# First layer of a four-layer attention stack: residual of the feed-forward on TensorE, GpSimd's norm between its energies, two buffers for low products

## What is computed

```
def layer_norm(x, g, b): return (x - mean) / sqrt(var + 1e-5) * g + b
Qh = (queries @ Wq).reshape(n, t, 16, 16).swapaxes(2, 3)
Kh = (keys @ Wk).reshape(n, t, 16, 16)
Vh = (values @ Wv).reshape(n, t, 16, 16).swapaxes(2, 3)
energy = jnp.matmul(Qh, Kh) / 8, and -1e+20 for masked tokens
attn = softmax(energy, axis=-1)
x = layer_norm(jnp.matmul(attn, Vh).reshape(n, t, 256) @ Wo + queries, ln1_g, ln1_b)
ff = relu(x @ W1 + b1) @ W2 + b2
return layer_norm(ff + x, ln2_g, ln2_b)
```

## Time and profile before

| | us |
|---|---|
| median of 3 runs | 2060.57 (2059.95 to 2061.29) |
| the profiled execution | 2058.21 |
| its span | 2056.5 |
| busy PE / PEld / DVE / ACT / POOL | 1810.5 / 1346.7 / 1258.3 / 1082.0 / 987.9 |
| first layer, from the start to about | 362 |
| mean granted TensorE clock, share of full speed | 0.928 |

### The profile page before, as it was taken

The page is one execution under the profiler, slowest core; times in us unless marked ns, Lnnn a source line. Parts: engine busy times, 40 slices in busy tenths (PEclk is TensorE's granted clock), DMA queues, the critical chain, the costliest instruction groups (busy, mean ns, idle before and its releaser), DMA issues.

```text
span 2056.5 us, 34737 instructions
## 1 busy us (share of the span) xinstructions
PE 1810.5 (88%) x12417; PEld 1346.7 (65%) x12417; DVE 1258.3 (61%) x2220; ACT 1082.0 (53%) x3150; POOL 987.9 (48%) x1233
## 2 busy tenths in 40 slices
PE   4777886879879978979999999999999999999997
PEld 3666675646646646656667767677676676766766
DVE  5878888574464464464465675756746547455471
ACT  2222221475576566566456565655655556656563
POOL 5666777564364355355244464535543334333340
PEclk8999998888978878887999999999999999999999
DMA  6300000000200000000000200000000000000000
GB/s 185 130 6 11 6 6 6 6 1 6 87 1 6 6 1 6 6 1 6 6 1 6 88 7 6 1 7 6 6 7 1 6 6 6 22 6 1 11 2 11
DMA packets 31361, 35.92 MB, mean 17 GB/s; under 512 B 3196, under 2 KB 30040, under 8 KB 30808
## 3 DMA queue, kind: packets, MB, share of 16 engines
q1 hardware_dynamic: 31192, 33.70, 5.3%
HBM read 31.60 MB, written 2.10 MB: 16 GB/s over the span
## 4 chain that ended last, share of the span: by engine, by line
PE 61%; DVE 14%; ACT 11%; POOL 6%; issue 5%; SPq 3%; DMA 1%; DVEq 0%; POOLq 0%; ACTq 0%
PE ps L590 34%; PE ps L794 6%; PE ps L732 6%; PE ps L804 5%; PE ps L838 4%; ACT work L972 3%; ACT work L979 3%; DVE work L1167 2%; PE ps L603 2%; POOL work L1360 2%; DVE xn L1026 2%; DVE rowmax L1171 2%; PE ps L753 2%; PE ps L819 2%; ACT hT L887 1%
## 5 line engine op out<-in xcount | busy, mean ns | idle before, releaser
L590 PE MATMUL ps<-hT,w_slot 128*128 128x256 f32 x1696 | 409.6, 395 | 18.2 <-ACT hT L887 16.1
L1284 POOL TENSOR_TENSOR work<-KT,own_head 128x512 f32<-128x512 f32 x256 | 262.5, 1047 | 286.8 <-PE ps L794 179.8
L590 PEld LDWEIGHTS ps<-hT,w_slot 128*128 128x128 f32 x1696 | 322.8, 196 | 78.6 <-ACT hT L887 21.7
L979 ACT ACTIVATE work<-work,rowmax 128x128 f32<-128x128 f32 x768 | 245.0, 392 | 168.2 <-DVE rowmax L1171 167.5
L804 PEld LDWEIGHTS ps<-ident,work 128*128 128x128 f32 x1536 | 198.9, 153 | 170.8 <-issue 89.0
L972 ACT ACTIVATE work<-ps,rowmax,score_scale 128x128 f32<-128x128 f32 x512 | 229.1, 488 | 114.5 <-DVE rowmax L1175 114.1
L804 PE MATMUL ps<-ident,work 128*128 128x128 f32 x1536 | 265.3, 301 | 18.3 <-ACT work L979 17.3
L794 PE MATMUL ps<-work,QT 128*128 128x512 f32 x512 | 266.4, 605 | 9.6 <-POOL work L1284 4.6
L1360 POOL TENSOR_SCALAR work<-work,winv 128x128 f32<-128x128 f32 x512 | 185.6, 383 | 159.0 <-DVE winv L1187 156.6
L1201 DVE RECIPROCAL O<-ps 128x128 f32<-128x128 f32 x128 | 122.3, 955 | 176.1 <-PE ps L838 175.4
L965 ACT ACTIVATE work<-ps 128x512 f32<-128x512 f32 x256 | 150.6, 595 | 91.2 <-PE ps L804 91.2
(11 more groups left out here) (129 smaller groups left out, 3290.3 us busy)
## 6 DMA issues: line engine op xcount, KB each, us to landing
ctx_in<-in_ctx SPq DMA_DIRECT2D x32, 256.0 KB, 2.7
w_slot<-in_L_xattn_W SPq DMA_DIRECT2D x2, 1024.0 KB, 6.4
w_slot<-in_L_xattn_ff_w SPq DMA_DIRECT2D x1, 2048.0 KB, 10.9
w_slot<-in_L_xattn_ffn_w SPq DMA_DIRECT2D x2, 1024.0 KB, 9.3
w_slot<-in_L_xattn_w SPq DMA_DIRECT2D x2, 1024.0 KB, 8.9
out<-x_all SPq DMA_DIRECT2D x8, 256.0 KB, 2.1
x_all<-in_x SPq DMA_DIRECT2D x1, 1536.0 KB, 11.7
pad<-in_mask_Bx1x1xS_fk SPq DMA_DIRECT2D x1, 1024.0 KB, 8.5
```

The costliest lines, as they stand in the source:

```text
L590: mm = pe.matmul(dst, lhsT(k), rhs(k), start=(k == 0), stop=(k == chunks - 1))
L979: ex = act.activation(prob[i % NPF][:, tok(h)], src[:, tok(h)], ACT.Exp, bias=shifts[:, at:at + 1])
L1284: pool.tensor_tensor(KB[u % NK].rearrange("p (h k) -> p h k", h=HU), keys, own_head[:, e:HC:2].unsqueeze(2).broadcast_to([P, HU, S]), ALU. ...
```

## The change

Four things, all in layer one. (1) The first norm's `post` and the `bias` step go; x after the first norm is no longer written. Its place as residual is taken by a piece `res`: four products of hT (x1 transposed, with g and b) with the identity, which open the PSUM accumulation of y2, and the second `sum` adds the row b2 to PSUM and writes x. (2) On GpSimd A1 moves from step 1 to step 4, so the first norm's two instructions come between A0 and A1; on TensorE E1 moves from step 3 to step 8, on VectorE W0 ahead of S1, on ScalarE the second exp from step 7 to 8. (3) Low products have two buffers: B0 writes `prodA`, B1 `prodB`. So B1 no longer waits for L0, B0 waits for E1 (`E_low_ps`), and A0 for L0 of the phase before. B1 moves from step 10 to 9. (4) The last `post` moves from slot 6 to slot 9. Two rows fewer are loaded.

```diff
@@ -33,8 +33,8 @@
     [("ctx", {}), ("stage", {}), ("tin", {}), ("local", {}), ("out", {"w": "Wo"}),
-     ("norm", {"eps": 1e-5}), ("post", {"g": "L0_ln1_g", "b": "L0_ln1_b"}), ("tin", {"g": "L0_ln1_g", "b": "L0_ln1_b"}),
-     ("bias", {"v": "L0_b2"}), ("ffn", {"w1": "W1", "b1": "L0_b1", "w2": "W2", "act": "relu"}),
+     ("norm", {"eps": 1e-5}), ("tin", {"g": "L0_ln1_g", "b": "L0_ln1_b"}),
+     ("ffn", {"w1": "W1", "b1": "L0_b1", "w2": "W2", "act": "relu", "res": "L0_b2"}),
      ("norm", {"eps": 1e-5}), ("post", {"g": "L0_ln2_g", "b": "L0_ln2_b"})],
@@ -73,7 +73,8 @@
         n = FC if arg["act"] == "geglu" else FC // 2
-        return [(f"f{f}", (f % 2 == 2 - 1) + 0 * (f == n - 1)) for f in range(n)] + [("y2", 0), ("sum", 1)]
+        res = [("res", 1)] if "res" in arg else []
+        return [(f"f{f}", f % 2 and not (res and f == n - 1)) for f in range(n)] + res + [("y2", 0), ("sum", 1)]
     if kind == "norm":
@@ -142,7 +143,7 @@
-LOCAL_LEFT_SLOT = {"norm": 4, "scale": 5, "post": 6}
+LOCAL_LEFT_SLOT = {"norm": 4, "scale": 5, "post": 9}
@@ -229,7 +230,7 @@
-ROWS = ["L0_ln1_g", "L0_ln1_b", "L0_b2", "L0_ln2_g", "L0_ln2_b", "L1_a1_bo", "L1_a2_bo", "L1_ff_b2",
+ROWS = ["L0_b2", "L0_ln2_g", "L0_ln2_b", "L1_a1_bo", "L1_a2_bo", "L1_ff_b2",
         "L2_mha1_bo", "L2_mha1_bv", "L2_ln1_g", "L2_ln1_b", "L2_mha2_bo", "L2_mha2_bv", "L2_ln2_g", "L2_ln2_b",
@@ -550,10 +551,11 @@
         LOCAL_STEPS = {
-            "pe": {2: [0], 3: [1]},
-            "act": {6: [0], 7: [1]},
-            "dve": {0: [("A", 0), ("R", 0)], 4: [("A", 1)], 5: [("R", 1), ("S", 0)], 6: [("S", 1)], 7: [("W", 0), ("B", 0)], 8: [("W", 1), ("L", 0)], 9: [("B", 1)], 10: [("L", 1)]},
-            "pool": {0: [("A", 0)], 1: [("A", 1)], 7: [("B", 0)], 10: [("B", 1)]},
+            "pe": {2: [0], 8: [1]},
+            "act": {6: [0], 8: [1]},
+            "dve": {0: [("A", 0), ("R", 0)], 4: [("A", 1)], 5: [("R", 1), ("S", 0)], 6: [("W", 0), ("S", 1)], 7: [("B", 0)],
+                    8: [("W", 1), ("L", 0)], 9: [("B", 1)], 10: [("L", 1)]},
+            "pool": {0: [("A", 0)], 4: [("A", 1)], 7: [("B", 0)], 9: [("B", 1)]},
         }
@@ -570,7 +572,7 @@
             x = DH // 2
-            prod = (prodD if half else prodB).rearrange("p (x h y) -> p x h y", x=x, h=H)
+            prod = (prodD if half else (prodA, prodB)[j]).rearrange("p (x h y) -> p x h y", x=x, h=H)
             e = E[:, j, half * P:(half + 1) * P].rearrange("p (x y) -> p x y", y=DH).unsqueeze(2).broadcast_to([P, x, H, DH])
@@ -585,9 +587,9 @@
-            def product(dst, lhsT, rhs, chunks):
+            def product(dst, lhsT, rhs, chunks, onto=False, more=False):
                 for k in range(chunks):
-                    mm = pe.matmul(dst, lhsT(k), rhs(k), start=(k == 0), stop=(k == chunks - 1))
+                    mm = pe.matmul(dst, lhsT(k), rhs(k), start=(k == 0 and not onto), stop=(k == chunks - 1 and not more))
                 return mm
@@ -724,6 +726,12 @@
                             mm.then_inc(q["hid_ps"], 1)
+                    elif piece == "res":
+                        pe.wait_ge(q["hid_ready"], FC * use("ffn", layer, g, n["ffn"]) + FC - 2)
+                        for j in range(G):
+                            for k in range(C):
+                                pe.matmul(one[:, j * D + k * P:j * D + (k + 1) * P], hT[st][:, k, tok(j)], ident[:, :],
+                                          start=(j == 0 and k == 0), stop=False)
                     elif piece[0:2] == "y2" and len(piece) == 3:
@@ -736,7 +744,8 @@
                         for j in range(G):
-                            mm = product(one[:, j * D:(j + 1) * D], lambda k: hid[:, k, tok(j)], lambda k: w[arg["w2"]][:, k, :], FC)
+                            mm = product(one[:, j * D:(j + 1) * D], lambda k: hid[:, k, tok(j)], lambda k: w[arg["w2"]][:, k, :], FC,
+                                         "res" in arg, "res" in arg and j < G - 1)
                         mm.then_inc(q["y_ps"], 1)
@@ -1028,7 +1037,10 @@
                         dve.wait_ge(q["y_ps"], use("yadd", layer, g, n["yadd"]))
-                        if n["bias"]:
+                        if "res" in arg:
+                            dve.wait_ge(s["rows_loaded"], 16 * len(ROWS))
+                        elif n["bias"]:
@@ -1039,6 +1051,8 @@
                                 .then_inc(q["yadd_done"], G)
+                        elif "res" in arg:
+                            dve.tensor_tensor(xs, y, row(arg["res"]).unsqueeze(1).broadcast_to([P, G, D]), ALU.add).then_inc(q["yadd_done"], G)
                         else:
@@ -1134,7 +1148,7 @@
                     dve.wait_ge(s["O_high"], G * (lp - 1) + j + 1)
-                    dve.tensor_reduce(O[st][:, j, 0:P], prodB.rearrange("p (e y) -> p e y", y=DH), AX.X, ALU.add).then_inc(s["o_ready"], 1)
+                    dve.tensor_reduce(O[st][:, j, 0:P], (prodA, prodB)[j].rearrange("p (e y) -> p e y", y=DH), AX.X, ALU.add).then_inc(s["o_ready"], 1)
@@ -1333,6 +1347,9 @@
+                        if j == 0:
+                            pool.wait_ge(s["o_ready"], G * (lp - 1) + 1)
                         for part in range(PARTS):
@@ -1341,7 +1358,10 @@
-                        pool.wait_ge(s["o_ready"], G * lp + j)
+                        if j == 0:
+                            pool.wait_ge(s["E_low_ps"], PARTS * (G * lp + G))
+                        else:
+                            pool.wait_ge(s["o_ready"], G * lp)
                         pool.tensor_tensor(*output_parts(st, j, 0), ALU.mult).then_inc(s["B_low"], 1)
```

## The result

The changed kernel takes **2109.64 us** (median, 2108.42 to 2112.34), the kernel before 2060.56 beside it: a ratio of **1.024**, 95% interval 1.0222 to 1.0258, 49 us slower where 40 were forecast. Its profiled execution took 2109.69 us, with a span of 2107.6, 51.1 more than before.

What follows compares the result with a forecast made beforehand. Waits bound layer one, along VectorE's chain fed by GpSimd. Phases 3 to 6 add 22.4 us, the others 1, 8, 6.5 and 2: 40 on the profiled 2058.2 gives 2098, with 2.4 for the median 2100; range 2072 to 2114.

Steps and rivals of the forecast that it cites:

- Norm between the energies: Layer-one phase: xn, held by GpSimd's A1, complete at 15.0 instead of 15.4; only 0.4 of 4.78 us wait comes back.
- TensorE's gap and its clock: TensorE ahead of xn: a gap of 5 us instead of 2.3, then 1.2 GHz costing 2.0 us.
- E1's end: TensorE in a layer-one phase: E1 ends at 26.5 us instead of 17.1.
- From E1 to the end of the phase: VectorE after E1: 17.0 us of work, 6.4 of holds and 0.2 for signals; phase 50.1, shaded to 49.8.
- hold of 4.1: VectorE at E1's end: S1's subtraction or xn stands 4.1 us behind GpSimd's B0, started on the same signal.
- that of 2.3: VectorE's B1 stands 2.3 us behind the rest of GpSimd's B1, which starts beside L0.
- rival 2: VectorE, S1 to L1: it gets in ahead of GpSimd, holds fall on GpSimd; 2045 to 2057 us, chance 0.12.
- What waits for E1: Layer-one phase: VectorE's S1, with xn and B0 queued behind it, and GpSimd's B0 wait for the later E1.
- Exp(1) ahead of the third chunk: ScalarE's exp(1) waits for S1, stopping TensorE some 3 us ahead of later hidden chunks, within slack.
- The residual: TensorE's identity products take 1.0 us, nothing where there is slack; removed post and bias could bring B0 forward some 4.
- The other phases: Layer-one phases outside 3 to 6 grow: number 0 by 1 us, 1 by 8, 2 by 6.5, 7 by 2.
- Layers two to four as before: A sign that the forecast is right: layers two to four stay as they were.

Runs made afterwards that it cites:

- b2: The change with GpSimd's A1 one step later, behind a wait for VectorE's xn: 2087.2 us, ratio 1.0129 to the kernel before.
- b3: The change with GpSimd's B0 and B1 on 2 of the 8 rows, other low outputs left out: 2068.3 us, ratio 1.0037 to the kernel before.
- a3: The change without its third part, both low products in one buffer with the old waits: 2076.2 us, ratio 1.0075 to the kernel before.
- b1: The change with its two buffers swapped, so B1 and not B0 waits for E1: 2076.1 us, ratio 1.0067 to the kernel before.
- a4: The change with TensorE's E1 back at step 3, ahead of the transposes: 2076.4 us, ratio 1.0076 to the kernel before.
- c1: The change with ScalarE's exp(1) behind the last hidden chunk: 2111.9 us, ratio 1.0262 to the kernel before.
- a1: The kernel before with only the residual part of the change, old order and one buffer: 2048.4 us, ratio 0.994.
- c2: The change with 22 useless matmuls on TensorE ahead of tin in layer one: 2094.7 us, ratio 1.0179 to the kernel before.
- b4: The change with 44 useless matmuls on TensorE ahead of tin in layer one: 2114.8 us, ratio 1.0261 to the kernel before.
- d1: c3 with 8 useless matmuls on TensorE ahead of tin: 2032.0 us, ratio 0.9865 to the kernel before.
- c3: The change with buffers swapped, GpSimd's A1 behind xn, E1 between tin and f0, W0 and exp(1) at old places: 2042.2 us, ratio 0.9926 to the kernel before.

## Why the prediction was right, step by step

- **Norm between the energies gives back little.** Right. Statistics end 7.4 us into phase 5 (7.5 said), the held instruction takes 2.13, rstd is there at 10.5 (10.7 said), xn is complete at 14.5 (15.0 said). That they end at 7.4 hangs on VectorE's A0, which I had not looked at. y ran at full rate (1.99 us) in phases 2, 4 and 5, but A0 is held by GpSimd's A0, now (3.46 at 304.79 against 2.28) and in the kernel before (3.68), so VectorE could not begin sooner. b2 shows what the hold of xn costs: 22 us.
- **TensorE's gap and its clock.** The mechanism was right, the size too small. The gap itself was 5.1 to 7.3 us (5 said), longest where y ran at full rate. f0 and f1 (tin excluded) took 6.32, 6.63, 5.10 and 6.03 us in phases 3 to 6, 6.0 on average and so 2.4 more than at full rate, and tin 0.5 more: 2.9, where the sum had 2.0. This is the term that failed in phases 3 to 6, which gained 6.1 us each (24.2) instead of 5.6 (22.4).
- **E1's end** at 26.5: 27.5, 27.2, 26.1 and 27.0 in phases 3 to 6, 0.45 later on average, which is the missing 0.5. It is small because errors cancel: the clock took 0.9 more, and the wait for hT behind tin 0.6 more (1.72 against the 1.11 of the earlier trace rows, a row of phase 7), but xn was there 0.5 sooner and E1 took 3.73 instead of 4.0.
- **From E1 to the end of the phase** 23.3: 23.2 in phase 5. The hold of 4.1 was 4.14 (on S1's subtraction), that of 2.3 was 2.34. GpSimd had the port first both times, so rival 2 had no place; b3, where 1.26 us of each holder is left, has phases of 44.3 (I had put 43.4 for no hold at all). This agrees with the Trainium skill, "SBUF — State Buffer", section "SBUF: two separate sides": the shared pair is locked for a whole instruction. Rows here add who comes next: the instruction that waits, even where the holder's engine goes straight on. The first xn ends right behind GpSimd's first product; the second (268.15) comes after GpSimd's second product has started (268.04) and is held until that ends, hence 3.82 for the two against 0.73. And when GpSimd went from B1 straight into its post (297.54), VectorE's waiting B1 ran first and the post took 3.34 us instead of 1.27, in all six phases that have one.
- **What waits for E1**, VectorE's S1 and GpSimd's B0, was named as the point of the prediction. a3 and b1 show B0's part (33 us), a4 that of the late E1 (33 us).
- **Exp(1) ahead of the third chunk** stops TensorE 2.77 us (3 said) in slack: right (c1).
- **The residual.** Its products cost nothing: right. The removed post and bias "would bring B0 forward by some 4 us if nothing new held it": in the old order that is worth 12 us (a1), which the change throws away.
- **The other phases.** Number 0: 1.0 (1 said). Number 1: 9.1 (8). Number 2: 7.1 (6.5). Number 7: 3.6 (2; 56.2 against 52.7), where the third xn took 2.56 beside a B0 of 5.99. Layer one in all: 44.9 against 40.
- **"Layers two to four as before"** put nothing there; between the two profiled executions it is 6.2 us, the larger part of the 11 that the profiled sum lacks. Their code is the same. Two stretches of layer two, first in the kernel before, then in the change:

```profile
631.50:789.00 157.50, 138.46 (x769) 98.06 (x768) 84.92 (x198) 96.48 (x323) 76.80 (x162) 0.83 0.02 4
789.00:948.00 159.00, 137.77 (x770) 98.18 (x769) 84.92 (x199) 96.74 (x324) 76.91 (x162) 0.84 0.02 4
```

```profile
679.50:840.00 160.50, 141.98 (x769) 100.02 (x768) 85.43 (x198) 97.16 (x323) 76.65 (x162) 0.81 0.01 4
840.00:1000.40 160.40, 141.91 (x770) 100.06 (x769) 85.41 (x198) 97.34 (x324) 76.64 (x162) 0.81 0.02 4
```

The same instructions, on TensorE 3.5 to 4.1 us longer, at a granted clock of 0.81 instead of 0.83 to 0.84. The column "rest" of the table gives the bound: over fourteen profiled executions with the same code there it goes from 1690.0 to 1696.1, the kernel before having the shortest and the change the longest (b2 and c2 are at 1696.0). It does not follow the first layer's time: a1, faster than before, has 1695.5, and b4, the slowest of all, 1692.9. But the kernel before by itself varies as much: its nine runs beside b1 have spans from 2054.3 to 2062.5 us, with a mean granted clock of 0.929 at the one end and 0.921 at the other, and its profiled execution (2056.5) is near the short end. So the 6.2 us are no more than two executions of one kernel can differ by, and nothing shows that the change made them. Where in the program those 8 us of the kernel before lie is not known, as only one of its executions was profiled.

## What to carry to other kernels

Ask of every new buffer whose last reader it waits for in the *new* order: two buffers were worth 11 us before the energies were moved and cost 33 after, and swapping their names gave those back. Where one signal, or the instruction just ahead, released a long GpSimd instruction beside short ones of VectorE, the short ones stood behind it: let GpSimd wait for them (b2) or have its work done before (b1). And count the clock in a gap's price: a gap of 4 to 7 us ahead of tin, f0 and f1 cost 2 to 3.5 us behind it, and useless matmuls that just fit the gap gave that back.

## What the runs showed that I had not expected

- Useless matmuls pay even in a gap of 2.1 us: 1.95 us of them took 2.2 us off E1 behind them (d1 against c3).
- A waiting VectorE instruction runs before the next one of GpSimd, although GpSimd goes straight on: the post behind B1 took 3.34 us instead of 1.27.
- A matmul of 128x128 in f32 counts as two records in the rows (44 as x88) of 0.114 us each; my estimate from a count of matmuls was half of what they took.
- Identical code in layers two to four takes 0.4% more or less, with the granted clock of layer two at 0.81 to 0.84, and one kernel's runs spread over 8 us; a difference of 6 us between two single profiles can lie outside all that was changed.
